# B and C rows on four column groups, PSUM sides exchanged by step, two gate tiles ahead of U's products

## The reference

```python
xc = silu(causal_conv4(x) + conv_b)          # x, gate = split(in_proj(h)), 1024 channels each
ssm_p = u @ x_proj_w.T                       # u = xc; 128 rows dt, 16 rows B, 16 rows C
delta = softplus(dt_lr @ dt_proj_w.T + dt_proj_b)
h = h * exp(d_t * A) + (d_t * u_t) * B_t     # for every t, 1024 channels x 16 states
y_t = sum over states of h * C_t
y = (y + u * D_param) * silu(gate)
out = y @ out_proj_w.T
# the FFN: down(silu(gate(x)) * up(x)), 512 -> 1376 -> 512, its weights looked up in a table of 16
```

## Time and profile before

| | us |
|---|---|
| median of 3 runs (lowest, highest) | 3514.39 (3513.63, 3516.52) |
| the profiled execution | 3514.81 |
| its span, first to last instruction | 3513.0 |
| step 0 (from its copy of dtl to the next step's) | 174.50 |
| steps 1 to 13, each | 173.56 to 173.58; step 8 173.70, step 9 173.93 |
| step 14 | 174.18 |
| step 15 with all that follows | 251.17 |

### The profile page before, as it was taken

The page is one execution under the profiler, slowest core; times in us unless marked ns, Lnnn a source line. Parts: engine busy times, 40 slices in busy tenths (PEclk is TensorE's granted clock), DMA queues, the critical chain, the costliest instruction groups (busy, mean ns, idle before and its releaser), DMA issues.

```text
span 3513.0 us, 46725 instructions
## 1 busy us (share of the span) xinstructions
PE 3235.1 (92%) x12672; PEld 2340.7 (67%) x12672; DVE 3142.4 (89%) x5676; ACT 2602.4 (74%) x5260; POOL 2472.9 (70%) x1959
## 2 busy tenths in 40 slices
PE   6898999899999999999999999999999999976738
PEld 5666766676776767676767676767677776754525
DVE  7899983699999999999999999999999999999990
ACT  6777773687878787878778787878787878766640
POOL 1434444496969696969696969696969696968680
PEclk9999999999999999999999999999999999988879
DMA  3222223111111111211111112021102120111110
GB/s 114 71 85 78 72 68 114 59 35 39 41 40 40 40 42 38 48 33 48 34 50 30 52 28 58 22 58 24 56 25 55 25 54 25 55 26 36 27 34 6
DMA packets 119380, 165.39 MB, mean 47 GB/s; under 512 B 8544, under 2 KB 84192, under 8 KB 118624
## 3 DMA queue, kind: packets, MB, share of 16 engines
q1 hardware_dynamic: 119136, 162.63, 16.4%
HBM read 128.39 MB, written 25.69 MB: 44 GB/s over the span
## 4 chain that ended last, share of the span: by engine, by line
POOL 45%; DVE 22%; issue 21%; PE 6%; ACT 4%; DMA 1%; DVEq 1%; POOLq 0%; SPq 0%; ACTq 0%
POOL dBu L921 24%; POOL yacc L934 17%; DVE D L1426 6%; DVE U L1375 4%; PE W L1176 3%; DVE prod L1445 2%; DVE dBu L1406 1%; DVE U L1418 1%; DVE D L1448 1%; PE W L1210 1%; DVE sgm L1359 1%; DVE delta L1413 1%; POOL NV L306 1%; POOL EO L294 1%; POOL MX L279 1%
## 5 line engine op out<-in xcount | busy, mean ns | idle before, releaser
L921 POOL TENSOR_TENSOR dBu<-U,BC 128x512 f32<-128x512 f32 x1024 | 1296.3, 1277 | 361.8 <-DMA BC<-bc_scratch 288.4
L1426 DVE TENSOR_TENSOR_SCAN D<-D,hc,dBu 128x256 f32<-128x256 f32 x2048 | 1432.2, 736 | 18.3 <-ACT D L1091 18.3
L1176 PE MATMUL W<-nT,wffn 128*128 128x256 f32 x5632 | 1231.6, 381 | 9.2 <-ACT nT L962 9.2
L1176 PEld LDWEIGHTS W<-nT,wffn 128*128 128x128 f32 x5632 | 1063.1, 189 | 183.9 <-issue 19.5
L1091 ACT ACTIVATE D<-delta,A 128x256 f32<-128x256 f32 x2048 | 891.0, 468 | 363.9 <-DVE yacc L1458 338.9
L934 POOL TENSOR_TENSOR yacc<-yacc,prod 128x512 f32<-128x512 f32 x752 | 956.7, 1272 | 176.5 <-DVE prod L1445 172.6
L1210 PE MATMUL W<-wffn,hT 128*128 128x512 f32 (+1 forms) x1408 | 617.5, 594 | 7.9 <-DVE hT L1344 7.9
L1445 DVE TENSOR_TENSOR prod<-D,BC 128x512 f32<-128x512 f32 x752 | 502.6, 668 | 0.0
L1176 PE MATMUL W<-nT,win 128*128 128x256 f32 x2048 | 452.5, 382 | 30.9 <-ACT xext L1010 23.7
L1210 PEld LDWEIGHTS W<-wffn,hT 128*128 128x128 f32 (+1 forms) x1408 | 262.9, 190 | 326.6 <-issue 307.8
L1176 PEld LDWEIGHTS W<-nT,win 128*128 128x128 f32 x2048 | 392.0, 192 | 92.9 <-ACT xext L1010 24.5
(11 more groups left out here) (128 smaller groups left out, 3037.8 us busy)
## 6 DMA issues: line engine op xcount, KB each, us to landing
BC<-bc_scratch SPq DMA_DIRECT2D x256, 256.0 KB, 4.6
XM<-x_scratch SPq DMA_DIRECT2D x29, 512.0 KB, 6.0
X<-x_scratch SPq DMA_DIRECT2D x17, 512.0 KB, 3.5
ix<-idx SPq DMA_DIRECT2D x33, 255.0 KB, 2.9
X<-x SPq DMA_DIRECT2D x16, 512.0 KB, 3.4
XR<-x SPq DMA_DIRECT2D x16, 512.0 KB, 3.4
x_scratch<-XR SPq DMA_DIRECT2D x16, 512.0 KB, 3.6
out<-X SPq DMA_DIRECT2D x16, 512.0 KB, 2.8
```

The costliest lines, as they stand in the source:

```text
L921: nc.gpsimd.tensor_tensor(dBu[e % 4][:], U[:, 2 * j:2 * j + 2, :], BC[slot][:, 0:1, :].to_broadcast([P, 2, CH]), ALU.mult).then_inc(s_dBu, 1)
L1176: last = T_.matmul(dst, lhsT, rhs, start=(n == 0), stop=(n == len(terms) - 1))
L1426: V.tensor_tensor_scan(D[:, m, :], D[:, m, :], dBu[e % 4][:, m % 2, :], hc[:, n, m:m + 1], ALU.mult, ALU.add).then_inc(s_scan, 1)
```

## The change

- B and C: the eight products with the 32 B/C columns of wx, accumulated today in one place (D[0:32, 6]), go to four groups of 32 PSUM partitions, k % 4, two products each; they are issued four at a time, after the dt products of quarters 1 and 3. ACT copies all 128 partitions to bcP; a product with `fold` (four stacked identities of 32 x 32, set up by POOL at the start) adds the four into D[0:32, 7]; it stands between the second and the third delta product. ACT copies bcS from there, and this copy now stands behind the table load.
- dtl and bcP lie in the two prod buffers, so ACT waits for POOL's last sum ahead of dtl, and DVE's first prod waits for the fold.
- Sides: `base(i)` exchanges W[0] and W[1] from step to step. Both halves of the gate go to different sides, so gate(1) needs only the windows copied, and no longer the first Silu of the gate.
- Two of the four tiles of gate(1) (`EARLY_GATES`) are made ahead of U's products, the other two behind the delta products.

```diff
...
+        fold = buf(ctx, "fold", [32])
...
+                nc.gpsimd.memset(fold[:], 0.0).then_inc(fold_set, 1)
+                for g in range(4):
+                    pool.wait_ge(fold_set, g + 1)
+                    nc.gpsimd.affine_select(out=fold[:], in_=fold[:], compare_op=ALU.not_equal, fill=1.0, base=-32 * g,
+                                            pattern=[[-1, 32]], channel_multiplier=1).then_inc(fold_set, 1)
...
-        dtl = buf(ctx, "dtl", [CH])
...
+        bcP, dtl = prod[0][:, 0, :], prod[1][:, 0, :]
...
-        SIDE_0, SIDE_EARLY, SIDE_LAST = 1, 0, 0
-
-        def side_late(f1):
-            return 1 - SIDE_EARLY if f1 else SIDE_EARLY
+        SIDE_0, SIDE_LAST = 1, 1
+
+        def base(i):
+
+
+            return min(i, NC - 2) % 2
+
+        def side_early(i):
+            return 1 - base(i)
+
+        def side_late(i, f1):
+            return base(i) if f1 else 1 - base(i)
...
-                    N_.activation(xext[:, 2 * q:2 * q + 2, KC - 1:], W[q // 2][:, a:a + 2, :], ACT.Copy).then_inc(m_ext, 1)
+                    N_.activation(xext[:, 2 * q:2 * q + 2, KC - 1:], W[(base(k) + q // 2) % 2][:, a:a + 2, :], ACT.Copy).then_inc(m_ext, 1)
...
-                        N_.activation(sgm[i % 2][:, 4 * h:4 * h + 4, :], W[0][:], ACT.Silu).then_inc(m_sg, 1)
+                        N_.activation(sgm[i % 2][:, 4 * h:4 * h + 4, :], W[(base(i) + h) % 2][:], ACT.Silu).then_inc(m_sg, 1)
...
+                    if back:
+                        act.wait_ge(s_acc, pool_sums(i))
                     act.wait_ge(m_dt, i + 1)
-                    N_.activation(dtl[:], D[:, 4, :], ACT.Copy).then_inc(m_dtl, 1)
+                    N_.activation(dtl, D[:, 4, :], ACT.Copy).then_inc(m_dtl, 1)
                     act.wait_ge(m_bc, i + 1)
+                    N_.activation(bcP, D[:, 6, :], ACT.Copy).then_inc(m_bcP, 1)
+
+                    N_.preload_act_table_set("natural_log_exp_and_others")
+                    act.wait_ge(m_fold, i + 1)
                     act.wait_ge(bc_stored, 16 * i)
-                    N_.activation(bcS[0:2 * S, :], D[0:2 * S, 6, :], ACT.Copy).then_inc(m_bcS, 1)
-
-                    N_.preload_act_table_set("natural_log_exp_and_others")
+                    N_.activation(bcS[0:2 * S, :], D[0:2 * S, 7, :], ACT.Copy).then_inc(m_bcS, 1)
...
-                def first_product(i, free, h_free):
+                def first_product(i, free):
 
                     pe.wait_ge(n_T, norm_no("M", i) + 1)
                     for h in range(2):
-                        if h == h_free:
+                        if h:
                             pe.wait_ge(*free)
                         for m in range(4 * h, 4 * h + 4):
-                            last = chain(W[h][:, m % 4, :], [(win[:, k, m * P:(m + 1) * P], nT[:, k, :]) for k in range(KH)])
+                            last = chain(W[(base(i) + h) % 2][:, m % 4, :], [(win[:, k, m * P:(m + 1) * P], nT[:, k, :]) for k in range(KH)])
...
                 def step(i, back, f1, more):
 
-                    def gate(h):
-
-                        for m in range(4 * h, 4 * h + 4):
-                            last = chain(W[0][:, m % 4, :], [(win[:, k, E + m * P:E + (m + 1) * P], nT[:, k, :]) for k in range(KH)])
-                        last.then_inc(m_g, 1)
+                    b = base(i)
+
+                    def gate(h, lo, hi):
+
+                        for m in range(lo, hi):
+                            last = chain(W[(b + h) % 2][:, m % 4, :], [(win[:, k, E + m * P:E + (m + 1) * P], nT[:, k, :]) for k in range(KH)])
+                        if hi == 4 * h + 4:
+                            last.then_inc(m_g, 1)
 
                     pe.wait_ge(m_ext, 4 * i + 2)
-                    gate(0)
+                    gate(0, 0, 4)
+
+                    pe.wait_ge(m_ext, 4 * (i + 1))
+                    gate(1, 4, 4 + EARLY_GATES)
                     pe.wait_ge(s_prod, NE * i)
                     pe.wait_ge(s_ha, pool_sums(i))
                     for q in range(ME // 2):
@@ -1257,40 +1284,43 @@
                             dt = T_.matmul(D[:, 4, :], wx[:, k, 0:R], U[:, k, :], start=(k == 0), stop=(k == ME - 1))
                         if q == ME // 2 - 1:
                             dt.then_inc(m_dt, 1)
-                        for k in (2 * q, 2 * q + 1):
-                            bc = T_.matmul(D[0:2 * S, 6, :], wx[:, k, R:R + 2 * S], U[:, k, :], start=(k == 0), stop=(k == ME - 1))
+                        if q % 2:
+                            for k in range(2 * q - 2, 2 * q + 2):
+                                g = k % 4 * 2 * S
+                                bc = T_.matmul(D[g:g + 2 * S, 6, :], wx[:, k, R:R + 2 * S], U[:, k, :], start=(k < 4), stop=(k >= 4))
                     bc.then_inc(m_bc, 1)
 
                     pe.wait_ge(m_dtl, i + 1)
                     for m in range(ME):
+                        if m == 2:
+                            pe.wait_ge(m_bcP, i + 1)
+                            pe.wait_ge(fold_set, 5)
+                            T_.matmul(D[0:2 * S, 7, :], fold[:], bcP, start=True, stop=True).then_inc(m_fold, 1)
                         if m == 6:
                             pe.wait_ge(m_bcS, i + 1)
-                        last = chain(D[:, m, :], [(wdt[:, m * P:(m + 1) * P], dtl[:])])
+                        last = chain(D[:, m, :], [(wdt[:, m * P:(m + 1) * P], dtl)])
                         if m % 2:
                             last.then_inc(m_dp, 1)
+                    gate(1, 4 + EARLY_GATES, 8)
                     pe.wait_ge(m_sg, 2 * i + 1)
-                    gate(1)
                     if back:
-                        pe.wait_ge(m_ext, 4 * (i + 1))
-                        project(i - 1, 0)
+                        project(i - 1, 0, b)
                     mamba = norm_no("M", i + 1) if more else None
...
                     if f1:
                         E_, L_ = ffn_no(*early(i)), norm_no(*early(i))
-                        turn(L_, SIDE_EARLY)
+                        turn(L_, side_early(i))
                         if back:
-                            project(i - 1, 1)
-                        else:
-                            pe.wait_ge(m_ext, 4)
-                        ffn(E_, L_, SIDE_EARLY, (m_res, i), L)
-                        ffn(F, L, 1 - SIDE_EARLY, (f_res, E_ + 1), mamba)
+                            project(i - 1, 1, b)
+                        ffn(E_, L_, side_early(i), (m_res, i), L)
+                        ffn(F, L, side_late(i, f1), (f_res, E_ + 1), mamba)
                     else:
-                        project(i - 1, 1)
-                        turn(L, SIDE_EARLY)
-                        ffn(F, L, SIDE_EARLY, (m_res, i), mamba)
+                        project(i - 1, 1, b)
+                        turn(L, side_late(i, f1))
+                        ffn(F, L, side_late(i, f1), (m_res, i), mamba)
                     if more:
-                        first_product(i + 1, (f_res, F + 1), side_late(f1))
+                        first_product(i + 1, (f_res, F + 1))
...
-                    resid(m_out, TT * (i + 1), X3, m_res, 1)
+                    resid(m_out, TT * (i + 1), X3, m_res, base(i + 1) if i + 1 < NC else 0)
...
+                            if r == 0:
+                                dve.wait_ge(m_fold, i + 1)
...
```

More of the change, by code:

```diff
@@ L34 @@
 AHEAD = 3
+EARLY_GATES = 2
 M_SUM = 50
@@ L108, in hybrid_block_kernel @@
         const_ready = sem("const_ready")
+        fold_set = sem("fold_set")
         ident_zero = sem("ident_zero")
@@ L1130, in step @@
                         if f1 and e == F1_EVAC:
-                            evac(norm_no(*early(i)), SIDE_EARLY)
+                            evac(norm_no(*early(i)), side_early(i))
                         if e == at["evac"]:
-                            evac(norm_no(*late(i)), side_late(f1))
+                            evac(norm_no(*late(i)), side_late(i, f1))
                         for p in range(NP):
                             if f1 and e == F1_SILU[p]:
-                                silu(ffn_no(*early(i)), norm_no(*early(i)), p, SIDE_EARLY)
+                                silu(ffn_no(*early(i)), norm_no(*early(i)), p, side_early(i))
                             if e == at["silu"][p]:
-                                silu(ffn_no(*late(i)), norm_no(*late(i)), p, side_late(f1))
+                                silu(ffn_no(*late(i)), norm_no(*late(i)), p, side_late(i, f1))
                         if more and e == min(at["m_evac"], NE - 1):
-                            evac(norm_no("M", i + 1), 1 - side_late(f1))
+                            evac(norm_no("M", i + 1), 1 - side_late(i, f1))
                     for j in range(4):
@@ L1221, in ffn, with project @@
                     last.then_inc(f_out, 1)
-                def project(i, t):
+                def project(i, t, side):
                     pe.wait_ge(wo_loaded, 16)
                     pe.wait_ge(m_y, 2 * (i + 1))
```

(14 more changed lines are left out.)

1 line of the change is left out of this document (added).

## The result

| | us |
|---|---|
| kernel before, median of 4 runs (lowest, highest) | 3514.06 (3513.63, 3516.52) |
| changed kernel, median of 4 runs (lowest, highest) | 3493.49 (3492.25, 3493.75) |
| ratio, 95% interval | 0.9939 [0.9923, 0.9954] |
| profiled execution, its span | 3493.3, 3491.5 |

0.6% faster, and 1.5 us from the forecast of 3495.0. Cut as before at the start of dtl's copy (now L1071), ten of the steps 1 to 13 last 171.73 to 171.98 us, steps 2, 6 and 7 last 172.43, 172.55 and 172.44; together 2235.5 against 2256.9. Step 0 lasts 174.19 and starts 0.6 later; step 14 lasts 173.42, step 15 with the rest 251.6. In this kernel's numbering gate tiles and delta products are L1197, dt L1284, B/C L1290, the fold L1298, bcP L1073, bcS L1078; in the run with direct B and C the two U products are L1282 and L1286.

A forecast was written before the change was run, and what follows sets the result against it. PE, through ACT's wait for the early FFN's first gate/up tile, sets the step period. Steps 1 to 13 -21.0, step 0 +1.6, steps 14 and 15 +0.1: total -19.3, about 3495 us from a profiled 3514.81; range 3484 to 3513.

The forecast's parts named there:

- The stall is PE's: DVE's stall before the second hT, early FFN: PE's lateness causes it; 2.67 falls to about 0.98, gain 1.69 us a step.
- Rival (b): The same stall is ACT's or another's, or PE is late for another tile: total +2.6, 3517 us; chance 0.12.
- The fold: Fold product behind the second delta product: costs PE 0.75 us (0.43 to 1.0), passed on by DVE's additions each step.
- POOL's start: POOL's first outer product starts later, 6.24 us after DVE's shifted first addition, so U times delta ends earlier: -0.68 a step.
- The steady step: Steps 1 to 13: +0.75 - 0.68 - 1.69 = -1.62 us each, -21.0 over thirteen.
- step 0: First step, PE without gaps: early tiles cost 3.45 us, shorter B/C work gives some back; +1.6 in all.
- Column groups: Eight B/C records on four groups: half overlap, about 1.1 us, first and last starts 0.9 apart; hidden in a steady step.
- (a): Rival: the four groups' B/C products don't overlap; total -12.4, 3502 us; chance 0.18.
- (c): Rival: column-group records don't even pipeline, 0.40 us each, eight take 3.2; total +12.3, 3527 us; chance 0.07.
- Early tiles free in a steady step: Two gate tiles ahead of U's products, 3.45 us: PE catches up by 1869.9, before the last quarter's U, costing nothing.
- The sides: Exchange of PSUM sides: adds no instruction, and each side's reader is done before its new writer.
- Steps 14 and 15: Last two steps, without early FFN, PE waiting for norms: +0.07 us each, +0.1 together.

The follow-up runs named there:

- e1: The changed kernel with no early gate tile, all four behind the delta products; groups, fold and sides stay: 3532.22 us, ratio 1.0051 to the kernel before.
- e4: The kernel before with only the exchange of PSUM sides; B and C as before, no early gate tile: 3514.40 us, ratio 1.0000.
- e2: The changed kernel with B and C projected directly, no column groups or fold, bcS copied before the table load: 3500.29 us, ratio 0.9961 to the kernel before.
- e5: e2 with the copy to bcS moved behind the table load: 3487.50 us, ratio 0.9921 to the kernel before.
- e9: The changed kernel with one early gate tile instead of two: 3518.61 us, ratio 1.0014 to the kernel before.
- e8: The changed kernel with three early gate tiles instead of two: 3493.57 us, ratio 0.9940 to the kernel before.
- e12: The changed kernel with ACT's last two skip products behind the softplus pairs and three early gate tiles, one in step 0: 3485.55 us, ratio 0.9922.

## Why the prediction was right, point by point

**The stall is PE's.** Confirmed for the larger part, by hT at 43.06, 41.33 and 40.46 with none, one and two tiles. The term was put at 1.69 with what remains of the stall at 0.98; it is 1.05, so that the stall itself shrank by 1.62. A third tile that gains nothing shows that the rest belongs to ACT and DVE. Rival (b) falls.

**The fold.** Put at 0.75: the third addition is 0.74 later, and e1's step is 0.75 over e4's.

**POOL's start.** Put at 6.24 behind the (shifted) addition and -0.68: by the rows above 2216.11 - 2208.99 - 0.74 = 6.38, and the last U product ends at 10.73 - 0.74 = 9.99, where 10.10 was forecast: -0.79. The mechanism is shown by e2 and e5, which differ in that copy's place alone. In steps 6, 8, 10 and 12 B and C land late and POOL is in DVE's way after all, at 0.2 to 0.8 a step; the forecast had nothing for that.

**The steady step.** 171.75 against 173.57 is -1.82, where -1.62 was forecast; with +0.74 and -0.79 the stall's term is what is left, -1.77. That is a remainder: 1.62 of it is read directly, the other 0.15 stands in no row shown. Times 13 that is -23.7, and -24.2 against the 2256.9 of before, which had 0.5 in steps 8 and 9. The halved clock gives 1.4 back, the late landings 1.4: -21.4 measured, -21.0 forecast. The sum is that near partly by luck: what was foreseen too small and what wasn't foreseen cancelled. In the whole span -21.5 came where -19.3 was forecast: 0.4 of the difference is the steady steps', 1.3 step 0's, 0.5 that of steps 14 and 15.

**Column groups.** This term was mis-sized. Half overlap was taken; it is all but full. The sign named for half overlap was first and last start 0.9 apart; they are 0.26 apart, two sets of four 0.24 behind each other, each set's starts within 0.02. In step 0 the next product starts 0.57 after the first. The Trainium skill's figure (TensorE: Matmul & The Clock Gate, Part 3), 2.38 for three column tiles of 512 elements a row, gives an estimate of 0.73; four groups of 256 did better here, at 0.64. In a steady step it is hidden, as forecast. In step 0 U's part got 3.18 shorter and not 1.9, so that steps and opening before step 1 cost 0.3 in place of 1.6. Rivals (a) and (c) fall with it.

**Early tiles free in a steady step.** Shown for the changed kernel: dt of the last quarter starts when its U is ready, with 1.25 us of pause ahead of it, and the first tile moves hT by its full length. But the cover was thinner than the forecast said: with direct B and C (e2) PE catches up nowhere, and the first addition comes 0.2 later.

**The sides.** No instruction, no time: e4. They are what lets the tiles go ahead, and they bring the turn behind ACT's second gate silu: the weight load of the turn waits 0.85 for it in step 9. Here the forecast's path was off. It left the silu's end where it was, 14.82 after dtl's copy, ahead of a turn at 15.05; the silu ended at 15.17 and the turn came at 15.23, behind it. In e1, e9 and e8, with none, one and three early tiles, it ends at 15.17 too in the undisturbed steps, and in e4, without the fold, at 14.82. The turn lost 0.2 by it, and this silu was the next bound.

**Steps 14 and 15.** +0.07 each was forecast; -0.76 and +0.4 came. In step 14 PE's tile is earlier there too (ACT's wait falls from 3.76 to 2.67); step 15 has the halved clock, some 1.4.

## What to carry to other kernels

When work is moved out of one engine's late stretch, it pays only until the next engine's own order holds, here about the middle of the second tile: try one dose less and one more. Work put into TensorE's pauses may pay by the clock as well, and the two are priced apart by doing it there and again where it was. Where VectorE and GpSimd both work from SBUF, a transfer that lands later can be the faster one, as in e5.

## What the runs showed of the hardware

The two things not expected: float32 products of 32 columns on four groups overlap to an extent that eight records end 0.64 us after the first starts (four starting within 0.02, four more 0.24 later), where four on one group take 1.05; and PE at half clock for 3.4 or 6.8 us at a time in a part where it pauses two to four times for ACT, which costs 0.7 to 1.9 us of the step in the changed kernel and e1, and up to 11 us in e1's steps 1 to 13. What brings it beyond the pauses is open. A halved stretch also followed a single pause of 2.55 us in four steps of e12, and not in nine others with the same pause.
